# Attention scores as products of 64 rows in the two halves of the partitions, with longer rings and new slots

## The reference, cut to what matters

```python
q = (h @ wq.T + bq_).reshape(bh, sl, H, DH)
k = (h @ wk.T + bk_).reshape(bh, sl, H, DH)
scores = jnp.einsum('blhd,bmhd->bhlm', q, k) * inv_sqrt_d
w_avg = jax.nn.softmax(scores, axis=-1).mean(axis=1)
new_w = jax.nn.softmax(CSCALE * w_avg + rel[None], axis=-1)
sa = jnp.einsum('blm,bme->ble', new_w, h)
h1 = _ln(h + sa, l1w, l1b)
h2 = _ln(h1, l2w, l2b)
ff = jax.nn.relu(h2 @ w1.T + b1_) @ w2.T + b2_
return (_ln(h2 + ff, l3w, l3b), None)
```

## Time and profile before

| what | value |
|---|---|
| median of 3 runs | 2652.36 us (2649.18 to 2653.47) |
| span of the profiled execution | 2651.5 us |
| PE matmul busy | 2528.1 us, 95% |
| ACT busy | 2422.1 us, 91% |
| DVE busy | 2414.4 us, 91% |
| POOL busy | 1516.9 us, 57% |
| DMA moved | 152.87 MB, mean 58 GB/s |
| first exponential of a score tile starts | 34.15 us |
| last exponential of a score tile ends | 2363.6 us |

### The profile page before, as it was taken

The page is one execution under the profiler, slowest core; times in us unless marked ns, Lnnn a source line. Parts: engine busy times, 40 slices in busy tenths (PEclk is TensorE's granted clock), DMA queues, the critical chain, the costliest instruction groups (busy, mean ns, idle before and its releaser), DMA issues. The chain is left out here.

```text
span 2651.5 us, 89129 instructions
## 1 busy us (share of the span) xinstructions
PE 2528.1 (95%) x35384; PEld 1185.5 (45%) x35384; DVE 2414.4 (91%) x5440; ACT 2422.1 (91%) x6760; POOL 1516.9 (57%) x1846
## 2 busy tenths in 40 slices
PE   5999999999999999999999999999999999999999
PEld 1344444444444444444444444444444344346887
DVE  6999999999999999999999999999999999984433
ACT  5999999999999999999999999999999999983232
POOL 3568856566566565664665655656656655544211
PEclk8999999999999999999999999999999999999999
DMA  4122222211212112122112122121121221200000
GB/s 132 58 77 68 74 71 71 66 46 54 69 42 84 57 54 63 49 70 66 46 60 64 46 84 68 54 64 48 54 83 44 65 62 38 66 19 5 28 17 24
DMA packets 98913, 152.87 MB, mean 58 GB/s; under 512 B 17856, under 2 KB 81088, under 8 KB 88896
## 3 DMA queue, kind: packets, MB, share of 16 engines
q1 hardware_dynamic: 97936, 146.26, 18.4%
q10 hardware_dynamic: 560, 0.92, 0.1%
HBM read 92.58 MB, written 41.94 MB: 51 GB/s over the span
## 5 line engine op out<-in xcount | busy, mean ns | idle before, releaser
L932 ACT ACTIVATE ex<-sc,negmax 128x512 f32<-128x512 f32 x3072 | 2125.0, 833 | 12.8 <-DVE negmax L729 8.9
L729 DVE TENSOR_REDUCE negmax<-sc 128x1 f32<-128x512 f32 x3072 | 1922.0, 673 | 18.1 <-PE sc L1064 12.8
L1064 PE MATMUL sc<-kb,qb 96*32 96x512 bf16 x12288 | 1077.2, 385 | 85.5 <-ACT ex L932 62.5
L932 ACT ACTIVATION_READ_ACCUMULATOR ex<-sc,negmax 128x1 f32 x3072 | 1082.8, 352 | 0.0
L1082 PE MATMUL mean<-ex,rw 128*32 128x512 f32 x6144 | 796.2, 593 | 7.5 <-ACT ew L938 7.5
L1064 PEld LDWEIGHTS sc<-kb,qb 96*32 96x32 bf16 x12288 | 319.9, 94 | 1005.8 <-ACT ex L932 883.4
L545 POOL TENSOR_TENSOR rw<-sel_sb,zinv 128x256 f32<-128x256 f32 x384 | 236.4, 616 | 661.8 <-DVE zinv L735 661.5
L1082 PEld LDWEIGHTS mean<-ex,rw 128*32 128x32 f32 x6144 | 186.5, 110 | 151.9 <-issue 72.8
L1071 PE MATMUL m<-hc,pt 128*32 128x129 f32 x6144 | 206.8, 275 | 0.0
L1071 PE MATMUL m<-h2t,w_sb 128*32 128x512 f32 x1536 | 201.5, 597 | 2.4 <-ACT relu L983 2.4
L1071 PE MATMUL m<-w_sb,relu 128*32 128x128 f32 x6144 | 201.3, 273 | 0.0
(11 more groups left out here) (124 smaller groups left out, 2425.5 us busy)
## 6 DMA issues: line engine op xcount, KB each, us to landing
kb<-qk_split SPq DMA_DIRECT2D x288, 128.0 KB
qb<-qk_split SPq DMA_DIRECT2D x568, 64.0 KB
qk_split<-kp SPq DMA_DIRECT2D x144, 128.0 KB, 1.9
qk_split<-qp SPq DMA_DIRECT2D x141, 128.0 KB, 1.8
hc<-hs SPq DMA_DIRECT2D x48, 256.0 KB, 2.8
xin<-x SPq DMA_DIRECT2D x16, 256.0 KB, 3.2
fh_raw<-fh SPq DMA_DIRECT2D x2, 1024.0 KB, 5.4
y_kept<-xin SPq DMA_DIRECT2D x8, 256.0 KB, 2.0
```

The lines of the kernel that those rows point to most:

```text
L729: nc.vector.tensor_reduce(negmax[:, s % RT:s % RT + 1], sc[s % NS][:, :], AX, ALU.max, negate=True) \
L932: nc.scalar.activation(ex[:, s % ET, :], sc[s % NS][:, :], ACT.Exp, bias=negmax[:, c:c + 1], accum_out=zsum[:, c:c + 1]).then_inc(exp_read ...
L1064: ins = nc.tensor.matmul(sc[s % NS][h * QS:h * QS + QS, :], qb[t % 2][:, h % 2, g, h // 2, r:r + QS], kb[t % 2][:, g, h // 2, :], start=Tr ...
```

## The change

Four things are changed together.

The score products are laid out anew. The six products of a feature now stand in groups of eight partitions (`SPREAD`), two of them zero, so that one head takes 64 partitions (`HALF`) and the two heads of a pair take the lower and the upper half. A score matmul reads only its head's 64 partitions of `qb` and of `kb`. The copy of `qb` with zeros goes, and with it half of the query transfers: six instead of twelve, each twice as large. In every second tile the heads are put into the output quarters in another order (`c ^ n % 2`), so that each output quarter comes from the lower half in one tile and from the upper in the next.

The memory that is given back goes to the rings: `ET` from 20 to 28, `RT` from 24 to 32. `ex` moves to another place in SBUF, and the final net takes other slots of it.

POOL sets four smaller tiles to zero at the start (`qb` and `kb`, two each, 128 partitions by half the length) in place of two.

All slots in `STEP` are set anew.

```diff
-ET = 20
-RT = 24
+ET = 28
+RT = 32
-ROWS = DH * NTERM
-LOADS = 3 * len(TERMS)
+SPREAD = 8
+HALF = DH * SPREAD
+LOADS = 2 * len(TERMS)
...
-    "sum_heads": (21, 23, 25, 26, 32, 33, 45, 50, 52, 56, 61, 64, 69, 71, 74, 75),
+    "sum_heads": (21, 21, 23, 26, 31, 35, 49, 51, 55, 55, 59, 61, 69, 72, 74, 75),
...
-    "up": (147, 150, 156, 158),
+    "up": (148, 152, 157, 159),
...
-        even_qb = att_sb("qb0", [2 * ROWS, 2, NG, 2, S], bf16)
-        kb = [att_sb(f"kb{i}", [2 * ROWS, NG, 2, S], bf16) for i in range(2)]
-        qb = [even_qb, att_sb("qb1", [2 * ROWS, 2, NG, 2, S], bf16)]
+        even_qb = att_sb("qb0", [P, NG, 2, S], bf16)
+        kb = [att_sb(f"kb{i}", [P, NG, 2, S], bf16) for i in range(2)]
+        qb = [even_qb, att_sb("qb1", [P, NG, 2, S], bf16)]
+        ex = att_sb("ex", [P, ET, S])
...
         def load_queries(queue, t, terms=range(NTERM)):
             for n in terms:
                 qs, _ = TERMS[n]
-                for hh in range(2):
-                    queue.dma_start(qb[t % 2][ROWS * hh + n:ROWS * hh + ROWS:NTERM, hh, :, :, :].rearrange("r g a s -> r (g a s)"),
-                                    qk_dram[SEQ[t], qs, P // 2 * hh:P // 2 * hh + P // 2, :].rearrange("(r g) s -> r (g s)", g=2 * NG)) \
-                        .then_inc(qk_loaded[t % 2], 16)
+                queue.dma_start(qb[t % 2][n:P:SPREAD, :, :, :].rearrange("r g a s -> r (g a s)"),
+                                qk_dram[SEQ[t], qs, :, :].rearrange("(r g) s -> r (g s)", g=2 * NG)).then_inc(qk_loaded[t % 2], 16)
...
-            gp.memset(qb[0][:, :, :, :, :].rearrange("r h g a s -> r (h g a s)").bitcast(f32), 0.0).then_inc(filled, 1)
-            gp.memset(qb[1][:, :, :, :, :].rearrange("r h g a s -> r (h g a s)").bitcast(f32), 0.0).then_inc(filled, 1)
+            for part in (qb[0], kb[0], qb[1], kb[1]):
+                gp.memset(part[:, :, :, :].rearrange("r g a s -> r (g a s)").bitcast(f32), 0.0).then_inc(filled, 1)
...
-                for h in range(HG):
-                    r = i * P + n * QS
-                    ins = nc.tensor.matmul(sc[s % NS][h * QS:h * QS + QS, :], qb[t % 2][:, h % 2, g, h // 2, r:r + QS],
-                                           kb[t % 2][:, g, h // 2, :],
+                r = i * P + n * QS
+                for c in range(HG):
+                    h = c ^ n % 2
+                    rows_h = slice(h % 2 * HALF, h % 2 * HALF + HALF)
+                    ins = nc.tensor.matmul(sc[s % NS][c * QS:c * QS + QS, :], qb[t % 2][rows_h, g, h // 2, r:r + QS],
+                                           kb[t % 2][rows_h, g, h // 2, :],
                                            start=True, stop=True)
```

More of the change, by code:

```diff
@@ L45 @@
 STEP = {
-    "invert_sums": (12, 17, 25, 36, 42, 55, 57, 66),
-    "row_weights": (18, 20, 30, 45, 48, 56, 66, 75),
-    "sum_heads": (21, 23, 25, 26, 32, 33, 45, 50, 52, 56, 61, 64, 69, 71, 74, 75),
[L49 to L62, removed]
-    "norm2_out": (142,),
-    "token_weight": (139,),
-    "token_bias": (174,),
-    "up": (147, 150, 156, 158),
[L67 to L81, removed]
+    "invert_sums": (15, 19, 26, 37, 45, 50, 58, 68),
+    "row_weights": (18, 20, 25, 40, 40, 49, 65, 68),
+    "sum_heads": (21, 21, 23, 26, 31, 35, 49, 51, 55, 55, 59, 61, 69, 72, 74, 75),
+    "exp_mean": (25, 49, 63, 74),
+    "transpose_mean": (30, 53, 73, 79),
+    "relative": (29, 55, 74, 78),
+    "attend": (40, 59, 78, 83),
+    "residual": (40, 66, 77, 83),
@@ new lines @@
+    "stats0": (75, 76, 82, 84),
+    "spread": (85, 100, 177),
+    "power": (85, 102, 172),
+    "apply0": (85, 87),
+    "norm1_weight": (92,),
+    "norm1_bias": (92,),
+    "stats1": (95, 95, 95, 99),
+    "apply1": (96, 107),
+    "norm2_turn": (144,),
+    "norm2_out": (142,),
+    "token_weight": (134,),
+    "token_bias": (159,),
+    "up": (148, 152, 157, 159),
+    "relu": (146, 152, 154, 158),
+    "down": (164, 166, 170, 173),
+    "add": (173,),
+    "stats2": (174, 174, 175, 175),
@@ L82 @@
+    "apply2": (182, 182),
+    "norm3_turn": (192,),
+    "norm3_out": (192,),
+    "norm3_weight": (183,),
+    "norm3_bias": (183,),
+    "project": (196, 203),
+    "queries": (201,),
+    "keys": (202,),
+    "split_q": (224, 224, 226, 232),
+    "split_k": (211, 220, 221, 235),
+    "last_weight": (187,),
     "last_bias": (193,),
[L83 to L86, removed]
+    "last_add": (194,),
+    "last_stats": (196,),
+    "last_spread": (199,),
@@ L87 @@
+    "last_power": (203,),
     "last_apply": (204,),
-    "last_turn": (204,),
-    "last_keep": (203,),
-    "first_stats": (3, 3, 5, 7),
+    "last_turn": (206,),
+    "last_keep": (204,),
+    "first_stats": (4, 5, 5, 10),
     "first_spread": (11,),
[L92 to L98, removed]
-    "first_keys": (55,),
-    "first_split_q": (65, 66, 69, 74),
@@ L101 @@
[L101 to L109, removed]
+    "first_power": (14,),
@@ new lines @@
+    "first_apply": (16, 16),
+    "first_turn": (48,),
+    "first_out": (45,),
+    "first_token": (39,),
+    "first_project": (49, 51),
+    "first_queries": (49,),
+    "first_keys": (55,),
+    "first_split_q": (60, 60, 63, 63),
+    "first_split_k": (55, 56, 75, 75),
+    "head_high": (2, 5, 5, 5, 5, 11, 23, 63),
+    "head_low": (6, 39, 58, 59, 59, 59, 59, 60),
+    "head_first": (63, 67, 70, 73, 74, 78, 86, 98),
+    "head_silu": (64, 67, 68, 71, 75, 78, 93, 99),
+    "head_gate": (63, 63, 74, 74, 76, 82, 103, 104),
@@ L110 @@
+    "head_square": (75, 80, 90, 93, 127, 127, 127, 140, 140, 140, 142, 146, 149, 155, 157, 221),
+    "head_gelu": (84, 86, 89, 124, 126, 130, 130, 130, 131, 139, 142, 142, 153, 172, 200, 203),
+    "head_split": (116, 117, 120, 120, 140, 142, 148, 159),
 }
-OLD = [(U * TILES + CH * i) % ET for i in range(2)]
+OLD = [(U * TILES + CH * i) % ET for i in range(4)]
 GROUPS = U + 1 + max(max(v) for v in STEP.values()) // TILES
@@ L189, in build @@
         parts.close()
-        ex = sb("ex", [P, ET, S])
         negmax = sb("negmax", [P, RT])
@@ L248, in build @@
         hid_lo = [sb(f"hid_lo{i}", [P, CH, S], f32r) for i in range(2)]
+        assert OLD[2:] == [0, CH]
+        sb("ex_rest", [P, ET - 2 * CH, S])
         fh_raw = sb("fh_raw", [P, CH, F])
@@ L330, in build @@
         KEPT = 16 * STORES
+        FILLS = 8
         def split_step(queue, engine, n, full, parts, part, done):
@@ L347, in load_keys @@
             for n, (_, ks) in enumerate(TERMS):
-                queue.dma_start(kb[t % 2][n:2 * ROWS:NTERM, :, :, :].rearrange("r g a s -> r (g a s)"),
+                queue.dma_start(kb[t % 2][n:P:SPREAD, :, :, :].rearrange("r g a s -> r (g a s)"),
                                 qk_dram[SEQ[t], 3 + ks, :, :].rearrange("(r g) s -> r (g s)", g=2 * NG)).then_inc(qk_loaded[t % 2], 16)
@@ L433, in _ @@
                 sp.dma_start(qk_dram[0, 3 + n, :, :], kp[n][:, :]).then_inc(kept, 16)
-            sp.wait_ge(filled, 7)
+            sp.wait_ge(filled, FILLS + 1)
             sp.wait_ge(q_kept, 48)
@@ L502, in _ @@
             gp.memset(eps4[:, :], EPS / 4).then_inc(filled, 1)
-            gp.memset(qb[0][:, :, :, :, :].rearrange("r h g a s -> r (h g a s)").bitcast(f32), 0.0).then_inc(filled, 1)
-            gp.memset(qb[1][:, :, :, :, :].rearrange("r h g a s -> r (h g a s)").bitcast(f32), 0.0).then_inc(filled, 1)
-            gp.wait_ge(filled, 6)
+            for part in (qb[0], kb[0], qb[1], kb[1]):
+                gp.memset(part[:, :, :, :].rearrange("r g a s -> r (g a s)").bitcast(f32), 0.0).then_inc(filled, 1)
+            gp.wait_ge(filled, FILLS)
             def power(k, n):
@@ L920, in _ @@
             first_copy(1)
-            act.wait_ge(filled, 7)
+            act.wait_ge(filled, FILLS + 1)
             act.wait_ge(q_kept, 48)
```

## The result

| | before | after |
|---|---|---|
| median | 2652.37 us (2649.18 to 2653.47, 4 runs) | 2773.18 us (2767.44 to 2774.63, 4 runs) |
| span of the profiled execution | 2651.5 us | 2770.0 us |
| first exponential of a score tile starts | 34.15 us | 30.94 us |
| last exponential of a score tile ends | 2363.6 us | 2478.7 us |

The changed kernel is slower by 4.5%: ratio 1.0451, 95% interval 1.0436 to 1.0465. The forecast was 2643, its range 2634 to 2697, so both value and direction were wrong. What happened is rival 1, with all its signs, and beside it a cost of the new slots that no rival had.

A forecast was written before the change was run, and what follows sets the result against it. ACT was taken as the bound; from the profiled 2651.5 us, 1.2 (start), 7 (ACT's idle time in units) and 1.5 (end) gave 2641.8, and with the median 0.9 above, about 2643 us; range 2634 to 2697.

The forecast's parts named there:

- rival 1: Units: mode changes between half-row score tiles and whole-row products make ACT late, 48 to 96 us, about 2715; chance 0.34.
- all its signs: Profile after: 0.3 or more from score tile to sum, unit 49.5 us or more, ACT waiting for DVE, DVE for PE.
- The bound: Inner units: ACT never stops, idle 0.17 us of 48.43 per unit; PE has 4.9 us to spare.
- the forecast's own range: Whole run: 2636 (first six units at reduced clock win as much as all others) to 2647 (ACT wins about 3).
- The start: Query transfers at kernel start: two of four before the first score tile go, saving 0.5 to 1.35 us, taken as 1.2.
- the row halves: Score tiles in units: 23 pairs start together, up to 4.6 us of PE; with freer slots 7.0 us for ACT.
- the longer pieces: Units: pieces of three and four tiles, lying elsewhere, catch up PE's lateness; argument against rival 1, no size given.
- The freer slots: New slots in units: with the row halves worth 0 to 0.17 us of ACT's idle time per unit, 0 to 7.5.
- The rings: Exponential of tile 44 in each unit: its wait for the sum over tiles 24 to 27 goes, alone worth nothing.
- The end: Final net: two of three 0.81 us waits before `up` go; 1.5 us less taken, between 0 and 2.5.

## Why the prediction was wrong, step by step

**The bound.** That ACT is the full engine, idle for 0.17 us per unit, and that only the start, this idle time and the end can be won, was right: the kernel with only the layout changed is at 2651.31, and the one with the statistics spread at 2649.56. What failed is that the same reading says nothing of how near PE is to becoming the bound. PE had 4.9 us of spare time per unit by my own count, but little of it where it was needed: in unit 24 of the kernel before (its first score tile starts at 1195.55) PE's first idle time stands at 1226.95, at tile 40.

```profile
1226.95 0.40 PE L1064 MATMUL sc<-kb,qb 96*32 96x512 bf16 x4 [0.27 <-ACT ex L932]
```

One reading of mine was wrong beside this: the low end of the forecast's own range leaned on six units with a reduced clock, while the earlier trace rows show it reduced in the first slice alone, 66 us.

**The start.** I took 1.2 us; it was 3.2. The two transfers that went saved 1.50 us of issue (1.20 instead of 2.70), but SP then stood 1.17 us before the key transfers, as the prediction had allowed for; the last of these was issued 1.32 us earlier (27.41 instead of 28.73). The rest is landing: the first score tile starts 29.48 - (23.68 + 3.73) = 2.07 us after that, before 32.68 - (24.40 + 4.33) = 3.95. Why the keys land sooner was not tried, and part of it may be chance: in the eleven traces of other kernels with this layout the first exponential starts at 31.10 to 32.64 us, and at 33.28 in the kernel before with its statistics spread.

```profile
21.31 1.20 SPq L358 DMA_DIRECT2D qb<-qk_split  x2
23.68 3.73 SPq L352 DMA_DIRECT2D kb<-qk_split  x6
...
29.48 1.47 PE L1067 MATMUL sc<-kb,qb 64*32 64x512 bf16 x20 [6.83 <-DMA kb<-qk_split]
```

**The failed step: the row halves, "between nothing and the whole 0.17 us per unit".** Pairs were to save up to 4.6 us of PE's time in a unit, and the changes between half rows and whole rows were left at zero in the sum. The pairs do run together; the run without them puts their worth at 2.0 us per unit on the clock. But 25 of the 31 pieces pay 0.22 us more than before for their way in and out (the 6 ahead of transposes paid already), 5.5 us per unit of PE's time, and in the dense half PE had little room for it. The forecast gave this cost to a rival, which took 0.2 per round trip from the earlier trace rows, the change between quarters and the whole array; that was nearly exact (0.22). I gave it only 0.34, for two reasons: that the longer pieces would catch up, and that a product of 96 rows and one of 128 follow each other at no cost. The first failed: the 1.6 us that ACT loses at tiles 10 to 22 of a unit are not made up later in it. The second isn't evidence on the question. The kernel with all 128 rows shows the same distance of 0.22 from score tile to sum, and 64 rows 0.33: here 96 rows behave as 128 do, and the changed kernel is the first to leave that group.

**The size of rival 1.** It expected 1 to 2 us per unit. ACT's idle time is now 2.6 us per unit: 0.78 at tile 10, 0.57 at tile 14, 0.25 at tile 22, 0.72 at tiles 46 to 48, 0.17 at tile 56. The 64 rows alone account for 1.5 us per unit (old slots), inside its bounds. The range was drawn too low for this rival: its 48 to 96 us begin at 2700, and the range ended at 2697.

**The slots.** "The freer slots" were priced between nothing and a gain. They cost 41 us without any change between rows. Some 15 of these went when the third `attend`, its residual and the transposes of the second norm stood in their old slots again. The line was in the table: the slot of `attend` went from 76 to 78, one ahead of slot 79. I counted PE's load by kinds and didn't follow which DVE result it needs next. Tiles 46 to 48 show the other form of this: each maximum of DVE has two statistics behind it, and ACT gets one tile in 0.98 us (1293.31 to 1294.29) instead of 0.67:

```profile
1291.61 0.68 DVE L730 TENSOR_REDUCE negmax<-sc 128x1 f32<-128x512 f32 x1
1292.21 0.47 DVE L691 BATCH_NORM_STATS2 bn<-xh 128x6 f32<-128x128 f32 x2
1292.60 0.67 DVE L730 TENSOR_REDUCE negmax<-sc 128x1 f32<-128x512 f32 x1
1293.19 0.47 DVE L691 BATCH_NORM_STATS2 bn<-xh 128x6 f32<-128x128 f32 x2
1293.59 0.67 DVE L730 TENSOR_REDUCE negmax<-sc 128x1 f32<-128x512 f32 x1
```

```profile
1293.31 0.69 ACT L933 ACTIVATE ex<-sc,negmax 128x512 f32<-128x512 f32 x1 [0.20 <-DVE negmax L730]
...
1294.29 0.69 ACT L933 ACTIVATE ex<-sc,negmax 128x512 f32<-128x512 f32 x1 [0.20 <-DVE negmax L730]
```

**The rings.** "Alone it is worth nothing" was nearly right: 7.6 us of 2719 where PE is late; it was not tried where PE isn't.

**The end.** The waits of 0.8 before each `up` are gone, and one stands before `down`, as forecast. The expected 1.5 us less became 3.4 more. New waits of 2.08 us (ahead of a block of `net_square`, at 2533.8 us) and 0.92 us stand elsewhere, where I had found none above a microsecond. And PE stood still for 2.36 us behind the last exponential (before 2.12); soon after, its granted clock was 0.50 of full speed, 1.2 GHz, for 3.4 us, where it had stayed full before. The first eight matmuls of the final net took 5.37 us, before 3.67.

```profile
2480.00:2483.40 3.40, 3.40 (x6) 1.34 (x5) 0.00 (x0) 1.60 (x2) 3.32 (x4) 0.50 0.00 0
```

```profile
2478.97 5.37 PE L1148 MATMUL sc<-hs,w_sb 128*128 128x512 f32 x8 [2.36 <-ACT ex L933]
...
2535.86 0.47 PE L1171 MATMUL sc<-hid_hi,fh_hi 128*128 128x512 f32 x1 [2.08 <-issue]
...
2562.75 1.52 PE L1074 MATMUL m<-w_sb,relu 128*32 128x128 f32 x48 [0.81 <-ACT relu L984]
```

## What to carry to other kernels

Before making some of the products smaller than the rest, count how often the two kinds take turns on PE and price each turn; where the trace has no such turn yet, take the price from another change of shape in it, which was right here. A saving inside the small products can be spent at their borders. Judge PE's spare time by the densest part of the period and not by its mean. And when slots are moved, follow each moved step to the next result that its engine waits for: here one `attend` two slots later, with two steps beside it, cost some 15 us.

## What I had not expected of the hardware

A change between products of 64 rows by 32 columns and of 128 rows by 32 columns costs PE 0.11 us in either direction (0.326 instead of 0.220, 0.542 instead of 0.428). That is as much as a score tile of 128 rows pays ahead of transposes of the whole array (0.325 instead of 0.216, median with all rows). A score tile of 64 rows ahead of transposes of the whole array pays this once, not twice: 1267.05 - 1266.72 = 0.33 us, no more than ahead of a sum. Two score tiles that use complementary quarters of the array cost 0.34 us together where one costs 0.33, and 0.54 when they use the same ones.

```profile
1266.72 0.40 PE L1067 MATMUL sc<-kb,qb 64*32 64x512 bf16 x4
1267.05 0.66 PE L1021 MATMUL m<-id_sb,h 128*128 128x128 f32 x4
```

The granted clock fell to half, 1.2 GHz, inside the late units too, which it did not do there before: for instance for 3.4 us at 2224.0 and again at 2275.2 us, where PE got through 24 matmuls in each stretch. Just ahead of 2224.0 PE had waited four times in a row for an exponential, 0.27, 0.27, 0.27 and 0.76 us.

```profile
2224.00:2227.40 3.40, 3.21 (x24) 0.44 (x24) 2.92 (x10) 3.40 (x12) 1.85 (x2) 0.50 0.62 198
...
2275.20:2278.60 3.40, 3.13 (x24) 0.44 (x24) 2.92 (x10) 3.39 (x11) 1.79 (x2) 0.50 0.68 198
```

The four units from 43 to 46 that contain such a stretch take 51.24 us instead of 50.93, so it explains 1 to 2 us of 118. What brings it about was not tried.
